# Layer 0's routing: gates behind the positions' sums, four row stores, more constant products

## The reference, cut to what matters

```python
macro_scores = jax.nn.sigmoid(xf @ macro_w)                     # 4 groups
mv, mi = _topk_normalized(macro_scores, GROUPS_TOP_K)           # 1 group: v / (v + 1e-9)
macro_full = jnp.sum(jax.nn.one_hot(mi, NUM_GROUPS) * mv[..., None], axis=1)
micro_scores = jax.nn.sigmoid(jnp.einsum('td,gde->tge', xf, micro_w))
uv, ui = _topk_normalized(micro_scores, TOP_K)                  # both experts of a group
w = (macro_full[:, :, None] * micro_full).reshape(T, NUM_EXPERTS)
gate = jax.nn.silu(jnp.einsum('td,edf->tef', xf, gate_w))
up = jnp.einsum('td,edf->tef', xf, up_w)
out = jnp.einsum('te,tef,efd->td', w, gate * up, down_w)
```

## Time and profile before

| What | Value |
|---|---|
| Median of 3 runs | 802.59 us (799.05 to 803.61) |
| Profiled execution, its own time | 797.08 us |
| Its span, first to last instruction | 795.2 us |
| Mean granted TensorE clock | 0.97 of full speed |
| Busy: TensorE, VectorE, ScalarE, GpSimd | 725.2, 454.4, 374.8, 356.0 us |
| Traffic over the span | 66.07 MB, mean 83 GB/s |
| 576 products in of layer 0 (L805) | 133.7 us busy, mean 382 ns |

### The profile page before, as it was taken

One profiled execution on the slowest core, in us unless ns is written; L12 is line 12 of the kernel. 1 busy time (PEld: TensorE's weight loads), 2 busy tenths in 40 slices (PEclk: granted clock), 3 DMA queues, 4 the chain that ended last, 5 costly groups with the idle time before them and its releaser, 6 DMA issues.

```text
span 795.2 us, 17663 instructions
## 1 busy us (share of the span) xinstructions
PE 725.2 (91%) x5661; PEld 587.5 (74%) x5662; DVE 454.4 (57%) x1205; ACT 374.8 (47%) x881; POOL 356.0 (45%) x310
## 2 busy tenths in 40 slices
PE   5989983999999999989898998889999999999991
PEld 4769863566666666667688987768888888888871
DVE  4898677343333433336788888935554554554540
ACT  5896667333333333333565765534434434444430
POOL 2539981132223222311586872043655556655331
PEclk9999996999999999999999999999999999999996
DMA  9970044041112211115322225412323233222225
GB/s 250 408 322 2 1 146 154 21 121 33 26 26 29 37 26 26 27 20 174 113 58 77 80 81 172 150 48 42 51 43 47 47 53 53 44 49 41 40 35 149
DMA packets 37180, 66.07 MB, mean 83 GB/s; under 512 B 3776, under 2 KB 29360, under 8 KB 35568
## 3 DMA queue, kind: packets, MB, share of 16 engines
q1 hardware_dynamic: 23696, 46.90, 17.7%
q0 software_dynamic: 13248, 18.21, 14.6%
q10 hardware_dynamic: 192, 0.38, 0.1%
HBM read 44.83 MB, written 23.35 MB: 86 GB/s over the span
## 4 chain that ended last, share of the span: by engine, by line
PE 69%; DVE 12%; POOL 8%; ACT 4%; DMA 3%; issue 2%; POOLq 0%; SPq 0%; DVEq 0%; ACTq 0%
PE PS L805 16%; PE PS L990 15%; PE PS L1003 15%; PE PS L823 8%; POOL X L1993 6%; PE PS L1362 3%; PE PS L813 3%; ACT Y L2017 1%; PE PS L1389 1%; DMA Y<-in_wtok_dram 1%; PE PS L975 1%; PE PS L1370 1%; POOL X L1988 1%; POOL X L1614 1%; DVE rs L2343 1%
## 5 line engine op out<-in xcount | busy, mean ns | idle before, releaser
L805 PE MATMUL PS<-X,Y 128*128 x576 | 133.7, 382 | 1.0 <-DVE Y L901 1.0
L1169 POOL DMA_INDIRECT sum<-X,dest x45 | 88.6, 1968 | 96.9 <-ACT X L1072 81.6
L1003 PE MATMUL PS<-X 128*128 x720 | 125.8, 273 | 1.9 <-ACT X L1072 1.9
L990 PE MATMUL PS<-X 128*128 128x256 f16 (+1 forms) x768 | 122.6, 265 | 0.4 <-issue 0.4
L1062 ACT ACTIVATE X<-PS,X 128x256 f32<-128x256 f32 (+1 forms) x192 | 72.8, 462 | 103.2 <-PE PS L990 100.1
L961 POOL DMA_INDIRECT sum<-Y,dest x24 | 38.0, 1585 | 148.8 <-ACT Y L878 148.8
L912 DVE SCALAR_TENSOR_TENSOR Y<-PS,Y 128x512 f32<-128x512 f32 x48 | 36.1, 751 | 116.1 <-PE PS L805 116.1
L805 PEld LDWEIGHTS PS<-X,Y 128*128 128x128 f16 x576 | 56.7, 98 | 60.0 <-issue 3.1
L990 PE MATMUL PS<-X,Y 128*128 128x256 f16 (+1 forms) x384 | 100.2, 264 | 0.0
L1003 PE MATMUL PS<-Y,X 128*128 x360 | 98.2, 273 | 0.0
L990 PEld LDWEIGHTS PS<-X 128*128 x768 | 71.7, 97 | 10.2 <-issue 0.9
(11 more groups left out here) (402 smaller groups left out, 1431.2 us busy)
## 6 DMA issues: line engine op xcount, KB each, us to landing
X<-in_w_dram SPq DMA_DIRECT2D x11, 1024.0 KB, 16.8
stage<-in_w_dram SPq DMA_DIRECT2D x16, 512.0 KB, 3.5
sum<-h SPq DMA_DIRECT2D x2, 2048.0 KB, 7.5
xs<-Y SPq DMA_DIRECT2D x2, 1040.0 KB, 6.3
xs<-Y SPq DMA_DIRECT2D x2, 1032.0 KB, 5.4
h<-in_txt_dram SPq DMA_DIRECT2D x2, 1024.0 KB, 18.1
Y<-in_patches_dram SPq DMA_DIRECT2D x3, 672.0 KB, 8.8
sum<-h SPq DMA_DIRECT2D x2, 768.0 KB, 6.4
```

Of the source, the lines that this page charges most:

```text
L805: ins = nc.tensor.matmul(PS[:, 2 * u + s, 0:F0], x_[:, slot, k, :], w_[:, at_:at_ + F0], start=(n == 0), stop=(n == 3 * KC - 1))
L990: ins = nc.tensor.matmul(PS[:, 2 * s + c // 2, (c % 2) * T1:(c % 2) * T1 + tokens], part[:, off:off + P], x_[:, slot, k, 0:tokens], start= ...
L1003: ins = nc.tensor.matmul(PS[:, 4 + a, 0:D], h_[:, s, c, a * P:(a + 1) * P], part[:, off:off + D], start=(s == 0 and c == 0 and n == 0), st ...
L1169: nc.gpsimd.indirect_dma_start(out=sum1, out_offset=bass.IndirectOffsetOnAxis(ap=dest[:, i:i + 1], axis=0), in_=y1buf[:, u % 2, i - first_ ...
```

## The change

Four edits, and the counts of semaphores that go with them.

1. The gates' 14 instructions, with the wait for the sigmoid and the `pay_ready` signal, become a function `row_gates`, which `positions` calls after its sums (behind L683) and before the position is split (L687). `full` (L656), which lay in `ra`, is put into `oh[:, 1]` for layer 0.
2. The last row store is split: 4 image tiles, then 2. The waits for the stores count 4 DMAs in layer 0 and 7 up to layer 1.
3. TensorE issues 30 constant products into bank 6 behind the scale's product, ahead of the experts.
4. TensorE issues 18 more between the first tile's transposes and its first product.

```diff
--- before.py
+++ after.py
@@ -76,6 +76,7 @@
 BY_ACT = range(6, XW0 // CW)
 HALVES = (0, 0, 2, 2, 1, 2, 2, 1, 2, 2, 1)
 GRAM = 256
+STORES0 = ((0, 8), (8, 8), (BATCH, 4), (BATCH + 4, IT - 4))
 NR = G0 + G0 * E0
 AHEAD = 2
 SAT = 17.0
@@ -634,7 +635,7 @@
             chain.link(nc.vector.tensor_tensor(to, spare[:, 0:tiles], to, ALU.subtract))
             chain.link(nc.vector.tensor_tensor(to, to, from_, ALU.add))
 
-        def positions(dve, chain, choices, tiles, done, inrow, intile, unit):
+        def positions(dve, chain, choices, tiles, done, inrow, intile, unit, meanwhile=None):
 
 
             hot = rc[:, 0:4, :]
@@ -653,7 +654,7 @@
             chain.link(nc.vector.tensor_tensor_scan(flat(upto), k_reset, flat(total), 0.0, ALU.mult, ALU.add))
 
             n_of = upto[:, :, NT - 1:NT].broadcast_to([P, 4, NFULL])
-            full = raf[:, 0:4 * NFULL].rearrange("p (g k) -> p g k", g=4)
+            full = (raf if done else oh[:, 1].rearrange("p g t -> p (g t)"))[:, 0:4 * NFULL].rearrange("p (g k) -> p g k", g=4)
             chain.link(nc.vector.tensor_tensor(full, n_of, k_fill[:, :, :], ALU.is_gt))
             tl, st, sl = sm[:, 0:4], sm[:, 4:8], sm[:, 8:12]
             over_tokens = lambda ap: ap.unsqueeze(2).broadcast_to([P, 4, NT])
@@ -681,6 +682,8 @@
             for c in range(choices):
                 chain.link(nc.vector.tensor_tensor(total, oh[:, c], before_, ALU.mult))
                 sum_over(chain, posf[:, c, :], total)
+            if meanwhile:
+                meanwhile()
 
 
             slots_of = posf[:, 0:choices, :]
@@ -833,6 +836,7 @@
                 w_ = weights(i)
                 if known(i, 0):
                     transpose_x(0, 0, 0)
+                    keep_clock(18, 6)
                 products_in(i, 0, w_, slot)
                 if not known(i, 0):
 
@@ -942,7 +946,7 @@
                     send(n - lag)
 
         def pool_slots0(pool):
-            pool.wait_ge(rows_stored, 48)
+            pool.wait_ge(rows_stored, 16 * len(STORES0))
             pool.wait_ge(source_ready, 1)
 
             def gather(n):
@@ -1144,7 +1148,7 @@
             base_y(UNITS1 - 1, expert_of(UNITS1 - 1))
 
         def pool_slots1(pool):
-            pool.wait_ge(rows_stored, 96)
+            pool.wait_ge(rows_stored, 16 * (len(STORES0) + 3))
             pool.wait_ge(source_ready, 2)
 
             def gather(n):
@@ -1179,11 +1183,11 @@
                 sp.dma_start(sum0[t * P:(t + n) * P].rearrange("(t p) n -> p t n", p=P), h[:, t:t + n, :])\
                     .then_inc(sum_based, 16)
             sp.wait_ge(pay_ready, 1)
-            for t, n in ((0, 8), (8, 8), (BATCH, IT)):
+            for t, n in STORES0:
                 sp.wait_ge(pay_normed, t + n)
                 sp.dma_start(xs0[t * P:(t + n) * P].rearrange("(t p) n -> p t n", p=P), pay[:, t:t + n, :])\
                     .then_inc(rows_stored, 16)
-            sp.wait_ge(rows_stored, 48)
+            sp.wait_ge(rows_stored, 16 * len(STORES0))
             sp.wait_ge(map_psum, 1)
             sp.wait_ge(y_done, 2)
             sp.dma_start(wqk, wattn[:, 0:2 * KC * D]).then_inc(attn_loaded, 16)
@@ -1233,6 +1237,7 @@
             pe.wait_ge(slots_ready, 1)
             pe.wait_ge(dest_ready, 1)
             pe_scale(pe, 0)
+            keep_clock(30, 6)
             pe_experts0(pe)
             pe_attention(pe)
             pe_layer1(pe)
@@ -1260,25 +1265,27 @@
             top, score, a, b = rc[:, 8, :], rc[:, 9, :], rc[:, 10, :], rc[:, 11, :]
             chain.link(nc.vector.tensor_scalar(rc[:, 0:4, :], ra[:, 0:4, :], SAT, None, ALU.min))
             first_max(chain, rc[:, 0:4, :], top, oh[:, 0], oh[:, 1], rc[:, 4:8, :])
-            dve.wait_ge(sig_ready, 1)
-
-            chain.link(nc.vector.tensor_reduce(score, rb[:, 0:4, :].rearrange("p g t -> p t g"), AX, ALU.max))
-            chain.link(nc.vector.tensor_scalar(a, score, 1e-9, None, ALU.add))
-            chain.link(nc.vector.reciprocal(a, a))
-            chain.link(nc.vector.tensor_tensor(score, score, a, ALU.mult))
-            u = ra[:, 0:2, :]
-            micro = rb[:, 4:12, :].rearrange("p (g e) t -> p e g t", e=E0)
-            for e in range(E0):
-                chain.link(nc.vector.tensor_tensor(rc[:, 0:4, :], micro[:, e], oh[:, 0], ALU.mult))
-                sum_over(chain, u[:, e, :], rc[:, 0:4, :])
-            chain.link(nc.vector.tensor_tensor(a, u[:, 0, :], u[:, 1, :], ALU.add))
-            chain.link(nc.vector.tensor_scalar(a, a, 1e-9, None, ALU.add))
-            chain.link(nc.vector.reciprocal(a, a))
-            chain.link(nc.vector.tensor_tensor(a, a, score, ALU.mult))
-            for e in range(E0):
-                chain.link(nc.vector.tensor_tensor(pay[:, :, D + e], u[:, e, :], a, ALU.mult))
-            dve.sem_inc(pay_ready, 1)
-            positions(dve, chain, 1, SLOT0, 0, inrow0, intile0, 1)
+            def row_gates():
+                dve.wait_ge(sig_ready, 1)
+
+                chain.link(nc.vector.tensor_reduce(score, rb[:, 0:4, :].rearrange("p g t -> p t g"), AX, ALU.max))
+                chain.link(nc.vector.tensor_scalar(a, score, 1e-9, None, ALU.add))
+                chain.link(nc.vector.reciprocal(a, a))
+                chain.link(nc.vector.tensor_tensor(score, score, a, ALU.mult))
+                u = ra[:, 0:2, :]
+                micro = rb[:, 4:12, :].rearrange("p (g e) t -> p e g t", e=E0)
+                for e in range(E0):
+                    chain.link(nc.vector.tensor_tensor(rc[:, 0:4, :], micro[:, e], oh[:, 0], ALU.mult))
+                    sum_over(chain, u[:, e, :], rc[:, 0:4, :])
+                chain.link(nc.vector.tensor_tensor(a, u[:, 0, :], u[:, 1, :], ALU.add))
+                chain.link(nc.vector.tensor_scalar(a, a, 1e-9, None, ALU.add))
+                chain.link(nc.vector.reciprocal(a, a))
+                chain.link(nc.vector.tensor_tensor(a, a, score, ALU.mult))
+                for e in range(E0):
+                    chain.link(nc.vector.tensor_tensor(pay[:, :, D + e], u[:, e, :], a, ALU.mult))
+                dve.sem_inc(pay_ready, 1)
+
+            positions(dve, chain, 1, SLOT0, 0, inrow0, intile0, 1, row_gates)
             dve_bound(dve, chain, dve_gram(dve, chain), lambda a_: None)
             dve_scale(dve, chain, 0)
             dve_experts0(dve, chain)
```

## The result

| | Before | Changed kernel |
|---|---|---|
| Median | 797.66 us (20 runs, 794.83 to 803.61) | 802.74 us (20 runs, 798.38 to 810.79) |
| Profiled execution, its span | 797.08, 795.2 us | 803.92, 801.9 us |

The ratio is 1.0055, 95% interval 1.0031 to 1.0080: +4.4 us, between +2.5 and +6.4. The change makes the kernel slower: the whole interval lies above no change. Whether it is past 0.5% is not settled, since 0.5% lies inside the interval.

The account below looks back on a forecast made before the run. Row stores of 2.91 MB, started by the gates and filling the DMA engines, were taken to bound the first gather. +3.20 (later landing), +0.07 (18 products) and zeros gave +3.3 us, 805.9 us, range 801.5 to 808.5.

Parts of the forecast that it names:

- rival 2: The 18 products between transposes and first product run at half clock, +0.96 for +0.07: +4.2 us, 806.8; chance 0.22.
- rival 1: Rows land later, but the fillers on both sides of TensorE's idling hold the clock: +1.6 us, 804.2; chance 0.17.
- Gates +3.20: VectorE, layer 0's routing: gates behind the positions' sums end at 127.89 instead of 124.69, +3.20 us.
- Landing +3.20, gather +3.20: Row stores wait for the gates: last landing at 138.83 for 135.63, gather at 139.26 for 136.06, +3.20 us.
- Positions worth nothing: VectorE's positions start 0.96 us earlier, `source` could come some 0.2 us earlier; covered by the store's landing, 0.
- Split 0: One more store issue on SyncE, made while the engines hold a backlog: 0, between nothing and 0.4 us.
- 30 products 0, 18 products +0.07, clock 0: TensorE: 30 run during the gather wait, 0; 18 before the first product, +0.07 us; clock falls, 0 of 1.68 won.
- Rival 3: The landing before the first gather follows ScalarE's last row alone, not the gates: -2.5 us, 800.1; chance 0.08.
- rival 4: The new last row store of 264 KB is slow, at 138 GB/s: +4.4 us, 807.0; chance 0.06.

Follow-up runs that it names:

- the run without gates: Before with the gate columns set to constant 0.5 and the stores' signal raised right behind the first choice; one execution, last landing at +15.77 us.
- 52 or 84: The changed kernel with 52 or 84 constant products in place of 30 behind the scale's product; ratio to before 1.0074 with 52, 1.0032 with 84.

## Why the prediction was right, step by step

It stood at +3.3 us, 805.9, with 801.5 to 808.5; measured were +4.4 (2.5 to 6.4) and 802.74. The base was 4.9 us too high: the three runs shown had a median of 802.59, twenty had 797.66. On the base of twenty the forecast would have been 801.0 and rival 2's +4.2 would have been 801.9. So it is the direction and the path of the loss that were right. The time itself was not: it is 3.2 us off the forecast, nearer to rival 1's 804.2, which the traces refute, and it was the width of the range that took it in.

- *Gates +3.20.* Measured +3.12.
- *Landing +3.20, gather +3.20.* Measured +3.15 and +3.01, and +3.24 and +3.11 with the gates alone. The reading of the full engines was right for later gates. As a statement on before it was half the truth: the sentence that the landing is set by when the first store starts missed the pace of ScalarE's rows as an equal limit, as the run without gates showed. The forecast did not suffer by it: where two limits are equal, a delay of either is paid in full. That they were equal was not foreseen, and is luck.
- *Positions worth nothing.* `source` came 0.45 us earlier (I had 0.2) and waited 4.4 us for the stores.
- *Split 0.* Within 0.2 us where it was made alone; with the constant products beside it and the gates where they were, the landing was 0.5 us later, which stays unexplained.
- *30 products 0, 18 products +0.07, clock 0.* The three add up to what was seen (+2.99 at the end, after +3.01 at the gather), but the last two were each wrong in the first profile: the 18 held the first product up by 0.87 us, as rival 2 has it, and the 12 products got 0.89 back. Half-clock time spent in the 18 was not spent in the products. In the second execution it was the other way round, 18 at full clock and 4.45 us for the 12. That the two errors cancel so closely was not foreseen. The windows show what lies behind it: the clock stood at half for 3.4 us in each of the four profiles of the two kernels (140.2 to 143.6 in the first of before, 144.7 to 148.1 here).
- *Rival 1* needed a bridge as long as the pause: with 52 or 84 the clock is held, and the pause that remained with 30 was 3.36 us (I had 2.96; the 30 ended 0.6 us earlier than I had worked out) or, in the second profile, 1.89. *Rival 2* has the number nearest to the measured +4.4, and half of its mechanism: the clock was at half before the 18, but the products behind them did not run at half for as long as before, so the stretch shows no +4.2. *Rival 3* fell with the gates alone; *rival 4* with the split alone.

The chance for slower by over 0.5% was 0.30, that for no such change 0.66; it came out at 0.55%, with an interval that holds both. The stretch explains 3.0 to 3.2 us in two pairs of profiles. The 1.2 to 1.4 us from there to 4.4 are within the interval and have no place that a profile shows; what lies behind the first product differs from one execution to the next by 2.6 us over all profiles (650.4 to 653.0), with no order by kernel.

## What to carry to other kernels

Ask of a step that is moved back what else it gates: here a signal at the end of the gates held the stores of 2.9 MB, which were longer than all that the step made room for. Where a transfer's last landing opens a stage, look for both its limits, the start of the first store and the pace of the engine that makes the rows; only a change that moves the later of them pays, and where they tie, both must move. In these runs constant products held the clock where they reached to within 0.5 us of the next work, and were in the way where they overshot: size them by the pause that is measured, and measure it more than once, since the same 30 left 3.36 us in one execution and 1.89 in another.

## What the runs showed that I had not expected

Small stores in a backlog were slow at a full busy share of the engines, 204 GB/s for stores of 129 KB where big ones had 349, and their issues, 0.5 to 0.7 us each, were not hidden either. The clock was held over a pause of 1.02 us without constant products where TensorE had idled only 0.32 us before the transposes (the run without gates, its 12 products in 2.76 us), while 1.5 to 1.6 and 1.0 us with the transposes between them let it fall in both profiles of before. In the run without gates the clock had also come back to full later, 17.5 us from the end of the first choice for 13.4 in before, so it is not shown that the pause alone decides.
